# Joining the end of a mixture-of-experts layer with the node stage of a graph attention layer, on one core

## The chip, the cores and the metric

The kernel runs on 1 core of one Trainium2 chip. The metric is the device time of one execution in microseconds (us); lower is better. The kernel before took 6367.42 us, the median of three runs (6361.59, 6367.42 and 6380.49). The core has a matrix engine (TensorE, PE in the profile; PEld is its loading of weights), VectorE (DVE), ScalarE (ACT), GpSimd (POOL), a queue engine that mostly issues DMAs (SP), an on-chip memory of 128 partitions, and PSUM, eight banks into which TensorE writes.

## The reference, cut to what matters

The program is a graph network: a gated graph layer, a first feed-forward layer with 8 experts, a graph attention layer, and a second feed-forward layer. The change touches the end of the first feed-forward layer and the start of the attention layer, for N = 3125 nodes of 256 values each.

```
H = gelu(layernorm(x) @ W1 + b1)            # 3125 x 1024
probs = softmax(H @ Wg + bg); e = argmax(probs)
x = x + probs[e] * (H @ Wd[e] + bd[e])      # one expert of 8 for each node
# attention layer, start
y = layernorm(x)
h = einsum('ni,hio->nho', y, W)             # 8 heads of 32 values
# for each edge: lin = hs.a1 + hd.a2 + (hd-hs).a3 + |hd-hs|.a4 + (hs*hd).a5
```

The kernel needs for every node its row h and two groups of eight numbers, worked out from products of y with weights and from half of a5 * h * h. It keeps h also as the sum of three bf16 parts (high, mid, low), with which later matmuls pick rows of nodes.

## The kernel before, in words

The nodes lie in 25 blocks of 128 (the last has 53), one row of a block in each partition. All engines run one program in stages. Between stages stands a join: every engine waits for the last semaphores of the stage. Inside a stage each engine has a fixed order of instructions, written out by Python loops, and waits on counting semaphores.

Experts stage (3693 to 3908.6 us in the trace). A routing part sorts nodes by expert into 32 tiles of 128 slots. For each tile POOL gathers 128 rows of H from DRAM (L1654), PE transposes them (L1680), ACT and DVE each copy half to SBUF (L1712, L1737), PE multiplies them with the expert's weights (L1695), DVE copies the product from PSUM (L1744) and SP stores it to `expert_rows` (L1645). Then, block by block, PE turns the block's gates (L1700), ACT copies them (L1718), PE multiplies them with the 8 x 256 biases (L1704) and DVE adds the result to X (L1748). Beside that POOL gathers the block's rows back from `expert_rows` (L1664, four buffers) and DVE multiplies them with the probability and adds them to X (L1751). A join follows.

Nodes stage (3908.6 to 3997.3 us). SP first stores the list of edge slots (L1801), loads the layer's weights (L1802 to L1806), and then issues the 16 DMAs of L1809. Each copies one row of 6658 numbers of `edge_sources` into 8 partitions of the tile PEN, which is 128 x 6658 f32 in the end; nothing reads it before the next stage. Meanwhile DVE and ACT do the layer norm for all 25 blocks (L928, L931, L944, L933, L935, then L938 on DVE and L948 on ACT write Y). DVE works out coefficients from the weights (L1872 to L1893). Then a loop over blocks: PE transposes Y (L1822), ACT copies that (L1843), PE multiplies it with 272 columns of weights into one of two PSUM banks (L1831), ACT copies the row h to HB (L1847), POOL multiplies it with half of a5 (L1865) and with itself (L1867), DVE sums that by head (L1900) and finishes the sixteen numbers (L1903, L1904). SP stores the block's row to `gat_rows` (L1812). ACT writes the high part (L1851), DVE the rest (L1916), ACT the mid part (L1855), DVE the low part (L1909).

The next stage starts after a join on, among others, all 25 stores of rows, all 25 low parts and the 16 loads of PEN:

```
join([ns["stored"](16 * NB), ns["low"](NB), ns["pen"](256), ns["zero"](1), ns["weights"](1), ns["slots"](16)])
```

Its first instructions are ACT's DMAs of L2045 and POOL's gathers of L1978.

Of the kernel before, what the change touches and what calls it, by code (L numbers as in the profile page):

```python
# [8 lines left out]
ALU = mybir.AluOpType  # L9
# [5 lines left out]
NB = 25  # L15
# [1428 lines left out]
def hidden_memory(ar, panels):  # L1444

    m = Box()
    m.Y = ar.mk(NB, D)
    m.yT = [ar.mk(2, 512) for _ in range(2)]
    m.gt = ar.mk(NB, 8)
# [6 lines left out]
    m.gT = ar.mk(128)  # L1456
# [10 lines left out]
    m.bd = ar.mk(256)  # L1467
# [5 lines left out]
HIDDEN = {"w": 80, "wd": 128, "ln_step": NB + 1, "ln_var": NB, "ln_sd": 1, "ln_nb": 1, "y_v": 15, "y_a": 10,  # L1473
# [5 lines left out]
def hidden_weights(q, a, m, s):  # L1479
    q.dma_start(m.W1[:, :, :], a["W1"].rearrange("(k p) n -> p k n", p=128)).then_inc(s["w"].sem, 16)  # L1480
    q.dma_start(m.b1c, a["b1T"]).then_inc(s["w"].sem, 16)
    q.dma_start(m.Wg[:, :, :], a["Wg"].rearrange("(k p) n -> p k n", p=128)).then_inc(s["w"].sem, 16)
    q.dma_start(m.bg, spread(a["bg"])).then_inc(s["w"].sem, 16)
    q.dma_start(m.bd[0:8], a["bd"]).then_inc(s["w"].sem, 16)
# [12 lines left out]
def hidden_tensor(t, m, s, PS, ident):  # L1497
    for q in range(NG):
# [14 lines left out]
        t.wait_ge(*s["w"](80))  # L1513
# [54 lines left out]
def hidden_vector(v, m, cn, s, st, PS):  # L1568
    ln_vector(v, m.ln, s, m.Y, m.X)
    for q in range(NG):  # L1570
# [6 lines left out]
        v.wait_ge(*s["w"](80))  # L1577
# [30 lines left out]
    st.mark(v.tensor_tensor(m.gt, m.OH, over(m.pmx), ALU.mult))  # L1608
    v.wait_ge(st.sem, st.n)
# [6 lines left out]
NYG = 4  # L1616


def experts_memory(ar):
# [12 lines left out]
    m.yg = [ar.mk(256) for _ in range(NYG)]  # L1632
# [5 lines left out]
           "gt_ps": NB, "gt_sb": NB, "bd_ps": NB, "bd": NB, "yz": 1, "yg0": 112, "yg1": 96, "yg2": 96, "yg3": 96,  # L1638
           "x_new": NB}
# [8 lines left out]
def experts_gpsimd(g, m, cn, s, HR, YS0):  # L1648
    g.memset(m.yg[(NB - 1) % NYG], 0.0).then_inc(s["yz"].sem, 1)
# [6 lines left out]
    g.wait_ge(*s["pos"](1))  # L1656
    g.wait_ge(*s["yz"](1))
    for i in range(2):
        g.wait_ge(*s[f"st{i}"](256))
    for b in range(NB):  # L1660
        n = rows_of(b)
        if b >= NYG:
            g.wait_ge(*s["x_new"](b - NYG + 1))
        g.indirect_dma_start(m.yg[b % NYG][0:n], None, YS0[:, :],  # L1664
                             bass.IndirectOffsetOnAxis(ap=m.r.posi[0:n, b:b + 1], axis=0)).then_inc(s[f"yg{b % NYG}"].sem, 16)


def experts_tensor(t, m, h, cn, s, PS, eregs):
# [29 lines left out]
    t.wait_ge(*s["tok"](1))  # L1698
    for b in range(NB):
        t.transpose(PS[0:8, 6, 0:128], h.gt[:, b, :], cn.ident).then_inc(s["gt_ps"].sem, 1)  # L1700
        t.wait_ge(*s["gt_sb"](b + 1))
        if b:
            t.wait_ge(*s["bd"](b))
        t.matmul(PS[:, 7, 0:256], lhsT=h.gT[0:8], rhs=h.bd[0:8], start=True, stop=True).then_inc(s["bd_ps"].sem, 1)  # L1704


def experts_scalar(c, m, h, s, PS):
# [6 lines left out]
    for b in range(NB):  # L1714
        c.wait_ge(*s["gt_ps"](b + 1))
        if b:
            c.wait_ge(*s["bd_ps"](b))
        c.activation(h.gT[0:8], PS[0:8, 6, 0:128], ACT.Copy).then_inc(s["gt_sb"].sem, 1)  # L1718


def experts_vector(v, m, h, cn, s, st, PS):
# [10 lines left out]
    for i in range(NT0 + 1):  # L1732
# [6 lines left out]
        if i >= 1:  # L1739
# [4 lines left out]
            v.tensor_copy(m.og[j % 2], PS[:, 4 + j % 2, 0:256]).then_inc(s["og"].sem, 1)  # L1744
    for b in range(NB):
        n = rows_of(b)
        v.wait_ge(*s["bd_ps"](b + 1))
        v.tensor_tensor(h.X[:, b, :], h.X[:, b, :], PS[:, 7, 0:256], ALU.add).then_inc(s["bd"].sem, 1)  # L1748
        v.wait_ge(*s["bd"](b + 1))
        v.wait_ge(*s[f"yg{b % NYG}"](16 * (b // NYG + 1)))  # L1750
        v.scalar_tensor_tensor(h.X[0:n, b, :], m.yg[b % NYG][0:n], h.pmx[0:n, b:b + 1], h.X[0:n, b, :],  # L1751
                               ALU.mult, ALU.add).then_inc(s["x_new"].sem, 1)
# [19 lines left out]
def nodes_memory(ar):  # L1772
# [3 lines left out]
    m.A = ar.mk(248)  # L1776
    m.a45 = ar.mk(4)
# [4 lines left out]
    m.Y = ar.mk(NB, D)  # L1782
    m.Wa = ar.mk(2, 272)
    m.av5 = ar.mk(5, 256)
    m.msk = ar.mk(8)
    m.yT = [ar.mk(2, 128) for _ in range(2)]
    m.u1 = [ar.mk(256) for _ in range(2)]
    m.u2 = ar.mk(2, 256)
    m.hq = ar.mk(8)
    m.R = [ar.mk(NROW) for _ in range(2)]  # L1790
    m.ln = ln_memory(ar)
    return m


NODES = {"w": 80, "pen": 256, "ln_step": NB + 1, "ln_var": NB, "ln_sd": 1, "ln_nb": 1, "y_v": 15, "y_a": 10, "coef": 1,
         "zero": 1, "weights": 1, "slots": 16, "yt_ps": NB, "yt": NB, "rows_ps": NB, "rows": NB, "square": 2 * NB, "hq": NB, "logits": 2 * NB,
         "high": NB, "rest": NB, "mid": NB, "low": NB, "stored": 16 * NB}


def nodes_sync(q, a, m, L, s, HD, SEGD, SLD):  # L1800
    q.dma_start(SLD.rearrange("(r n) o -> r (n o)", r=104), L.slT[0:104]).then_inc(s["slots"].sem, 16)  # L1801
# [5 lines left out]
    for r in range(16):  # L1807
        row = SEGD[r * LROW:(r + 1) * LROW + 2, 0]
        q.dma_start(m.PEN[8 * r:8 * r + 8, :], row.unsqueeze(0).partition_broadcast(8)).then_inc(s["pen"].sem, 16)  # L1809
    for b in range(NB):  # L1810
        q.wait_ge(*s["logits"](2 * b + 2))
        q.dma_start(HD[b * 128:(b + 1) * 128, :], m.HB[:, b, 8:272]).then_inc(s["stored"].sem, 16)  # L1812


def nodes_tensor(t, m, s, PS, ident):
    for i in range(NB + 1):
        if i < NB:
            t.wait_ge(*ln_ready(s, i))
# [5 lines left out]
        if i >= 1:  # L1824
# [3 lines left out]
            if b >= 2:  # L1828
                t.wait_ge(*s["logits"](2 * b - 2))
            for k in range(2):  # L1830
                ins = t.matmul(PS[:, b % 2, 0:272], lhsT=m.yT[b % 2][:, k, :], rhs=m.Wa[:, k, :],  # L1831
# [4 lines left out]
def nodes_scalar(c, m, s, PS, epsc):  # L1836
    ln_scalar(c, m.ln, s, m.Y, m.X, epsc)
# [1299 lines left out]
```

## Time and profile before

| | |
|---|---|
| median of three runs | 6367.42 us (6361.59 to 6380.49) |
| the profiled execution | 6372.08 us, its span 6370.7 us |
| experts stage, tile loop | 3711 to 3858.8 us |
| experts stage, biases and gathers back | 3858.8 to 3908.6 us |
| nodes stage, layer norm and coefficients | 3908.6 to 3930 us |
| nodes stage, loop over blocks | 3930 to 3997.3 us |

Times inside the span are counted from its start. A row of the timeline tells the start, how long, the engine, the line of the kernel, the operation, what it writes and reads, how many were merged, and in brackets how long the engine had been idle and what released it. The granted clock (PEclk) is a share of TensorE's 2.4 GHz: 1.00 is 2.4 GHz and 0.50 is 1.2 GHz. "SPq" and "ACTq" are DMA issues; their time is the issue, not the transfer.

### The profile page before, as it was taken

The numbers are of one execution on the slowest core, as the hardware profiler recorded it, in microseconds if no ns is written. First come the engines' busy times: TensorE is split into PE (matmuls) and PEld (weight loads), VectorE is DVE, ScalarE is ACT, GpSimd is POOL, SyncE is SP. The second block draws the span as 40 slices with busy tenths as digits, with TensorE's granted clock in tenths as the row PEclk, the third lists the DMA queues.
The fourth block names the chain that finished last, engine by engine and source line by source line (L and its number), as shares of the span: only waits on it lengthen the run. The fifth ranks groups of instructions, "written<-read, shape, count | busy, mean of one in ns | idle before, by whom it ended". The sixth has DMA issues, their size and how long they took to land. (4 is left out here: it accounts for less than half of the span.)

```text
span 6370.7 us, 62334 instructions
## 1 busy us (share of the span) xinstructions
PE 4485.8 (70%) x17114; PEld 2672.2 (42%) x17114; DVE 2768.0 (43%) x6269; ACT 1760.5 (28%) x4039; POOL 2391.3 (38%) x2828
## 2 busy tenths in 40 slices
PE   1111314258999999999998986577777775997794
PEld 0010101024544544544444464455555554664462
DVE  7994000023263344353214035444444447777435
ACT  4331000000000000000001312345454455997121
POOL 3787777710000000000001013666666663886024
PEclk9999655579899999999999997688888887998697
DMA  8700122137432221322333133566666663776323
GB/s 356 286 1 25 58 75 75 58 125 260 137 110 92 89 96 71 111 83 74 109 111 105 66 125 90 174 201 199 196 197 202 196 195 99 241 242 215 116 63 107
DMA packets 381089, 865.14 MB, mean 136 GB/s; under 512 B 87347, under 2 KB 187733, under 8 KB 353370
## 3 DMA queue, kind: packets, MB, share of 16 engines
q1 hardware_dynamic: 250281, 686.15, 30.7%
q0 software_dynamic: 76816, 147.75, 9.0%
q10 hardware_dynamic: 53664, 27.26, 1.5%
q8 instruction: 159, 2.61, 0.2%
q14 instruction: 169, 1.38, 0.1%
HBM read 576.84 MB, written 284.11 MB: 135 GB/s over the span
## 5 line engine op out<-in xcount | busy, mean ns | idle before, releaser
L1110 PE MATMUL PS<-mem 128*128 128x512 f32 (+1 forms) x3500 | 1465.5, 575 | 392.4 <-issue 258.5
L1110 PEld LDWEIGHTS PS<-mem 128*128 128x128 f32 x3500 | 655.7, 201 | 1177.3 <-issue 1037.3
L1978 POOL DMA_INDIRECT mem<-gat_rows,mem x832 | 811.3, 975 | 479.9 <-issue 451.3
L1291 POOL TENSOR_TENSOR mem<-mem 128x256 f32<-128x256 f32 x25 | 19.9, 833 | 2140.5 <-DMA mem<-x 2140.5
L581 POOL DMA_INDIRECT adjacency_more<-mem x526 | 543.4, 1033 | 171.1 <-issue 171.1
L2086 DVE TENSOR_TENSOR mem<-mem,PS 128x512 f32<-128x512 f32 x416 | 285.7, 687 | 673.3 <-ACT mem L2059 516.2
L2021 PE MATMUL PS<-mem 128*128 128x256 bf16 x2496 | 437.1, 309 | 176.8 <-issue 163.3
L1176 ACT ACTIVATE mem<-PS 128x512 f32<-128x512 f32 (+1 forms) x35 | 19.0, 544 | 1918.0 <-PE PS L1110 1359.6
L2326 PE MATMUL PS<-mem 128*128 128x264 f32 x1660 | 461.6, 406 | 7.6 <-DVE mem L2283 3.1
L262 PE MATMUL PS<-mem 106*128 106x106 f32 (+4 forms) x446 | 102.0, 374 | 476.9 <-DVE mem L393 302.9
L1220 DVE COPY mem<-PS 128x512 f32<-128x512 f32 (+1 forms) x35 | 21.9, 625 | 954.0 <-PE PS L1110 651.3
L2059 ACT ACTIVATE mem<-PS,mem 128x256 f32<-128x256 f32 x832 | 424.1, 560 | 13.8
L2054 ACT ACTIVATE PS<-PS 128x512 f32<-128x512 f32 x416 | 245.2, 590 | 651.2 <-remote 507.8
L2021 PEld LDWEIGHTS PS<-mem 128*128 x2496 | 269.7, 109 | 276.7 <-issue 226.8
L581 POOL DMA_INDIRECT adjacency<-mem x256 | 347.3, 1357 | 95.4 <-issue 80.0
L2013 PE MATMUL PS<-mem 128*128 128x128 f32 x1664 | 311.0, 309 | 100.5 <-issue 77.8
L2326 PEld LDWEIGHTS PS<-mem 128*128 128x128 f32 x1660 | 283.3, 190 | 185.8 <-DVE mem L2283 92.8
L1993 PE MATMUL PS<-mem 128*128 128x256 f32 x832 | 330.7, 487 | 42.3 <-issue 34.9
L2283 POOL TENSOR_TENSOR mem<-mem 128x256 f32<-128x256 f32 x415 | 267.8, 645 | 166.6 <-ACT mem L2184 81.6
L2013 PEld LDWEIGHTS PS<-mem 128*128 128x128 f32 x1664 | 243.0, 162 | 168.0 <-issue 130.1
L1245 DVE TENSOR_TENSOR mem<-mem 128x2560 f32<-128x2560 f32 (+1 forms) x35 | 86.5, 2485 | 476.0 <-DMA mem<-adjacency_more 316.9
L2307 ACT ACTIVATE mem<-mem 128x128 f32<-128x128 f32 x830 | 287.9, 394 | 13.5
(398 smaller groups left out, 7033.3 us busy)
## 6 DMA issues: line engine op xcount, KB each, us to landing
mem<-adjacency SPq DMA_DIRECT2D x150, 1280.0 KB
gathered_rows<-mem SPq DMA_DIRECT2D x416, 264.0 KB
mem<-gathered_rows SPq DMA_DIRECT2D x208, 528.0 KB, 4.6
adjacency<-mem SPq DMA_DIRECT2D x56, 800.0 KB, 20.7
adjacency_more<-mem SPq DMA_DIRECT2D x56, 800.0 KB
mem<-adjacency_more SPq DMA_DIRECT2D x30, 1280.0 KB
adjacency<-mem SPq DMA_DIRECT2D x30, 1280.0 KB
mem<-edge_slots ACTq DMA_DIRECT2D x26, 1024.0 KB
```

The source lines that it names most:

```text
L581: g.indirect_dma_start(AD[:, :], bass.IndirectOffsetOnAxis(ap=aidx[:, k:k + 1], axis=0), SF[:, k:k + 1], None).then_inc(sc[f"{name}{n % 2} ...
L1110: ins = t.matmul(PS[:, f, 0:n], lhsT=h[:, b, f * 128:(f + 1) * 128], rhs=m.pan[i % NPAN][:, j, 0:n], start=(b == 0), stop=(b == NB - 1))
L1978: g.indirect_dma_start(m.Dg[i % RING][:, k, j, :], None, HD[:, :], bass.IndirectOffsetOnAxis(ap=L.idxD[:, c:c + 1], axis=0)).then_inc(s[f" ...
L1993: ins = t.matmul(PS[:, 7, 0:256], lhsT=nd.A[:, 120 - a:248 - a], rhs=m.x[p % NXD], start=(p % 16 == 0), stop=False)
L2013: t.matmul(PS[:, bank, f * 256 + e * 128:f * 256 + e * 128 + 128], lhsT=rows[:, e, f * 128:f * 128 + 128], rhs=cn.ident, is_transpose=True ...
L2021: t.matmul(PS[:, bank, f * 256:f * 256 + 256], lhsT=parts[:, bass.ds(at * 99 + (part * NROW + 8 + f * 128), 128)], rhs=slots, start=False, ...
L2054: c.activation(d, d, ACT.Abs).then_inc(s["ab"].sem, 1)
L2059: c.activation(m.by[n % 3][:, f * 256:f * 256 + 256], d[:, f * 256:f * 256 + 256], ACT.Identity, bias=nd.a45[:, f:f + 1], scale=nd.a45[:, ...
L2086: v.tensor_tensor(m.xx[n % 2], m.by[n % 3], PS[:, n % NDT, :], ALU.mult).then_inc(s["xx"].sem, 1)
L2283: return e.tensor_tensor(m.Wv[i % NOUT][:, j, 0:256].rearrange("p (f h d) -> p f h d", f=2, h=8), m.Dg[k % NDG][:, 2 * (i % 2) + j, 0:256] ...
L2307: c.activation(m.Ab[n % 2][:, j, :], cn.iota, ACT.Abs, bias=L.nsl[:, 2 * n + j:2 * n + j + 1]).then_inc(s["ab2"].sem, 1)
L2326: ins = t.matmul(PS[:, (6, 7, 0, 1)[i % NOUT], 0:264], lhsT=m.On[i % NOUT][:, j, :], rhs=m.Wv[i % NOUT][:, j, :], start=(j == 0), stop=(j ...
```

## The change

The two stages become one without a join between. The biases are no longer made by PE: a copy of all 8 x 256 biases is loaded into every partition before the tile loop, and DVE adds the right one while it evicts a tile's product; the tile's expert number is read into registers. In the new stage DVE adds a gathered block to X, works out its mean and variance at once, and the standard deviations are made for groups of five blocks. ACT alone writes Y. The squares of a row come from ACT, straight from PSUM, and POOL is left with one multiplication a block. There are six PSUM banks for products, four buffers for squares and rests, and 25 areas for gathered rows. These areas and the biases lie in tile AT, and some weights lie where PEN will be; so the 16 DMAs into PEN now stand behind the seventeenth store of rows and behind a wait for the last x_new. The coefficients are worked out in the tile loop, at its fifth step. The weights' loads stand ahead of the tile loop.

```
-            v.tensor_copy(m.og[j % 2], PS[:, 4 + j % 2, 0:256]).then_inc(s["og"].sem, 1)
+            if j % 8 == 0:
+                v.reg_load(regs, m.eo[0:1, j:j + 8])
+            e = v.snap(regs[j % 8], min_val=0, max_val=7 * 8)
+            v.tensor_tensor(m.og[j % 2], PS[:, 4 + j % 2, 0:256], nd.bd[:, bass.ds(e * 32, 256)],
+                            ALU.add).then_inc(s["og"].sem, 1)
+        if i == 4:
+            nodes_coefficients(v, nd, ns, st)
```

The loops for the biases on PE (L1700, L1704), ACT (L1718) and DVE (L1748) are removed, and in the hidden stage the load of the biases and one small multiplication on DVE (L1608).

```
+    m.yg = [m.AT[:, 256 * b:256 * b + 256] for b in range(NB)]
+    m.bd = m.AT[:, 0:2048]
+    m.av5 = m.PEN[:, 0:1280].rearrange("p (a b) -> p a b", a=5)
+NU = 4
+NBANK = 6
+ROWS_AT, REST_AT, LOW_AT = 9, 12, 15
+GATHERS_AHEAD = 10
...
+def nodes_sync(q, m, L, s, HD, SEGD, SLD):
     for b in range(NB):
         q.wait_ge(*s["logits"](2 * b + 2))
         q.dma_start(HD[b * 128:(b + 1) * 128, :], m.HB[:, b, 8:272]).then_inc(s["stored"].sem, 16)
+        if b == NB - ROWS_AT:
+            q.wait_ge(*s["x_new"](NB))
+            for r in range(16):
+                row = SEGD[r * LROW:(r + 1) * LROW + 2, 0]
+                q.dma_start(m.PEN[8 * r:8 * r + 8, :], row.unsqueeze(0).partition_broadcast(8)).then_inc(s["pen"].sem, 16)
...
 def nodes_tensor(t, m, s, PS, ident):
     for i in range(NB + 1):
         if i < NB:
-            t.wait_ge(*ln_ready(s, i))
+            t.wait_ge(*s["y"](i + 1))
             (transposes of block i; then, for i >= 1, the products of block i - 1)
...
 def nodes_scalar(c, m, s, PS, epsc):
+    deviations(0)
+    for i in range(NB + 8):
         if i < NB:
+            c.wait_ge(*s["nb"](i // 5 + 1))
+            c.activation(m.Y[:, i, :], m.X[:, i, :], ACT.Identity, bias=m.ln.nb[:, i:i + 1],
+                         scale=m.ln.sd[:, i:i + 1]).then_inc(s["y"].sem, 1)
             c.wait_ge(*s["yt_ps"](i + 1))
...
+            c.activation(m.HB[:, b, 8:264], PS[:, b % NBANK, 0:256], ACT.Copy).then_inc(s["rows"].sem, 1)
+            c.activation(m.u1[b % NU], PS[:, b % NBANK, 0:256], ACT.Square).then_inc(s["square"].sem, 1)
...
+        if i % 5 == 4 and i + 1 < NB:
+            deviations(i // 5 + 1)
...
+def nodes_gpsimd(g, x, m, s, es, YS0):
+    for b in range(NB + GATHERS_AHEAD):
+        if b < NB:
+            (gather block b, from b = 5 on after x_new of block b - 5)
+        if b >= GATHERS_AHEAD:
+            k = b - GATHERS_AHEAD
+            g.wait_ge(*s["square"](k + 1))
+            g.tensor_tensor(u, u, m.a5h, ALU.mult).then_inc(s["fifth"].sem, 1)
...
+def nodes_vector(v, h, m, s, es, PS):
+    for i in range(NB + LOW_AT):
+        (block i: x_new, bn_stats, bn_aggr; at i = 5, 10, ...: reciprocal and nb of a group)
+        (low part of block i - 15; sums and sixteen numbers of block i - 9; rest of block i - 12)
```

SP's order. Of the kernel before, from the last stores of the tile loop to the end of the nodes stage:

```order
L1645 DMA expert_rows<-mem 128x256 x32
L1801 DMA edge_slots<-mem 104x1024
L1802 DMA mem<-Wgat 128x2x256
L1803 DMA mem<-a 128x1280
L1804 DMA mem<-a4c 128x2
L1805 DMA mem<-a5c 128x2
L1806 DMA mem<-c_mask 128x8
L1809 DMA mem<-edge_sources 8x6658 x16
L1812 DMA gat_rows<-mem 128x264 x25
```

The same place of the changed kernel:

```order
L1785 DMA mem<-bd 128x2048
L1786 DMA mem<-Wgat 128x2x256
L1787 DMA mem<-a 128x1280
L1788 DMA mem<-a4c 128x2
L1789 DMA mem<-a5c 128x2
L1790 DMA mem<-c_mask 128x8
L1637 DMA expert_rows<-mem 128x256 x32
L1794 DMA edge_slots<-mem 104x1024
L1797 DMA gat_rows<-mem 128x264 x17
L1803 DMA mem<-edge_sources 8x6658 x16
L1797 DMA gat_rows<-mem 128x264 x8
```

The weights moved ahead of the stores of the tile loop, and the loads of `edge_sources` moved from ahead of all 25 stores of rows to behind the seventeenth.

ACT's order in the loop over blocks. Of the kernel before, a block's four instructions (turned Y, row, high part, mid part):

```order
L1843 ACTIVATE mem<-PS 128x256
L1847 ACTIVATE mem<-PS 128x256
L1851 ACTIVATE mem<-mem 128x264
L1855 ACTIVATE mem<-mem 128x264
L1843 ACTIVATE mem<-PS 128x256
```

Of the changed kernel, the deviations of a group (L1831) and one block (Y, turned Y, row, square, high part, mid part):

```order
L1831 ACTIVATE mem<-mem 128x5
L1837 ACTIVATE mem<-mem 128x256
L1842 ACTIVATE mem<-PS 128x256
L1846 ACTIVATE mem<-PS 128x256
L1849 ACTIVATE mem<-PS 128x256
L1854 ACTIVATE mem<-mem 128x264
L1858 ACTIVATE mem<-mem 128x264
```

Y of a block (L1837) and the square (L1849) moved into ACT's loop. PE's order in the loop is the same in both: two transposes of block i, then two products of block i - 1.

## Rows read from the trace of the kernel before

**Rows 1.** Windows: microseconds, busy of each engine (instructions), clock, DMA share, GB/s.

```profile
3858.80:3908.60 49.80, 36.48 (x74) 13.99 (x74) 22.62 (x51) 6.41 (x24) 24.46 (x25) 0.54 0.23 67
3925.70:3930.00 4.30, 0.00 (x1) 0.04 (x1) 4.09 (x12) 0.73 (x3) 0.00 (x0) 0.50 0.55 87
3955.00:3975.00 20.00, 14.02 (x51) 9.89 (x48) 12.76 (x40) 10.90 (x32) 12.56 (x16) 0.83 0.28 89
```

**Rows 2.** Timeline of the queue SP, 3680 to 4010 us.

```profile
3911.37 5.85 SPq L1809 DMA_DIRECT2D mem<-edge_sources  x16
```

**Rows 3.** Timeline, the last eviction, the first gathers, the end of the stage.

```profile
3858.40 0.42 DVE L1744 COPY mem<-PS 128x256 f32<-128x256 f32 x1 [3.04 <-PE PS L1695]
3861.29 0.95 POOL L1664 DMA_INDIRECT mem<-expert_rows,mem  x1 [21.68 <-DMA expert_rows<-mem]
3862.55 0.95 POOL L1664 DMA_INDIRECT mem<-expert_rows,mem  x1 [0.30 <-issue]
...
3864.12 0.49 DVE L1751 SCALAR_TENSOR_TENSOR mem<-mem 128x256 f32<-128x256 f32 x1 [4.14 <-DMA mem<-expert_rows,mem]
3864.53 0.42 DVE L1748 TENSOR_TENSOR mem<-mem,PS 128x256 f32<-128x256 f32 x1
...
3996.25 1.00 DVE L1909 TENSOR_TENSOR mem<-mem 128x264 bf16<-128x264 f32 x2
```

**Rows 4.** Timeline, the layer norm of the nodes stage.

```profile
3908.65 8.27 DVE L928 BATCH_NORM_STATS2 mem<-mem 128x6 f32<-128x256 f32 x25
...
3916.83 1.75 DVE L931 BATCH_NORM_AGGREGATE mem<-mem 128x2 f32<-128x6 f32 x25
...
3918.66 1.28 ACT L944 ACT_TABLE_LOAD   x1 [12.29 <-DVE mem L931]
...
3920.87 4.54 ACT L948 ACTIVATE mem<-mem 128x256 f32<-128x256 f32 x9 [0.60 <-DVE mem L935]
```

**Rows 5.** Source L948: instructions, ns minimum/median/maximum, first and last start.

```profile
L948 ACT ACTIVATE mem<-mem x40: 585/587/602, 556.5 to 5885.5; 128x256 f32<-128x256 f32 x40
```

**Rows 6.** Timeline of the loop over blocks, three places.

```profile
3931.94 0.63 PE L1822 MATMUL PS<-mem 128*128 128x128 f32 x2
...
3934.43 0.38 ACT L1847 ACTIVATE mem<-PS 128x256 f32<-128x256 f32 x1 [1.43 <-PE PS L1831]
...
3955.33 0.36 ACT L1843 ACTIVATE mem<-PS 128x256 f32<-128x256 f32 x1
...
3955.59 0.38 ACT L1847 ACTIVATE mem<-PS 128x256 f32<-128x256 f32 x1
...
3961.50 0.41 ACT L1855 ACTIVATE mem<-mem 128x264 bf16<-128x264 f32 x1
3961.82 0.37 ACT L1843 ACTIVATE mem<-PS 128x256 f32<-128x256 f32 x1
```

**Rows 7.** Windows, columns as in rows 1.

```profile
3866.00:3906.00 40.00, 32.52 (x65) 12.24 (x64) 19.28 (x43) 5.61 (x21) 20.67 (x21) 0.50 0.25 71
4009.00:4017.00 8.00, 4.40 (x23) 3.12 (x22) 7.36 (x5) 3.20 (x6) 7.70 (x2) 0.50 0.23 82
3930.00:3935.00 5.00, 4.82 (x12) 3.27 (x12) 0.65 (x3) 1.15 (x3) 1.57 (x3) 0.52 0.44 69
```

**Rows 8.** DMA issues, 3908 to 3998 us: KB each, median us to landing.

```profile
mem<-edge_sources SPq DMA_DIRECT2D x16, 208.1 KB
gat_rows<-mem SPq DMA_DIRECT2D x25, 132.0 KB, 1.8
```

**Rows 9.** Windows, columns as in rows 1.

```profile
3918.00:3919.00 1.00, 0.00 (x0) 0.00 (x0) 0.58 (x9) 0.34 (x1) 0.00 (x0) 0.50 0.53 80
3962.00:3963.00 1.00, 0.88 (x5) 0.51 (x3) 0.04 (x1) 0.49 (x2) 0.84 (x2) 0.97 0.08 23
```

**Rows 10.** Timeline of the tile loop.

```profile
3737.72 0.42 DVE L1744 COPY mem<-PS 128x256 f32<-128x256 f32 x1 [2.78 <-PE PS L1695]
...
3742.74 3.63 PE L1695 MATMUL PS<-mem 128*128 x16
```

More of the change, by code:

```diff
@@ L1637 @@
            "tr_ps": 2 * NT0, "cp_a": NT0, "cp_v": NT0, "mm": NT0, "og": NT0, "st0": 256, "st1": 256,
[L1638 to L1639 removed]
+           **{f"yg{i}": 16 * NB // NYG for i in range(NYG)}}
 def experts_sync(q, m, s, YS0):
@@ L1713, in experts_scalar, with experts_vector @@
                      ACT.Copy).then_inc(s["cp_a"].sem, 1)
[L1714 to L1721, printed above, removed]
+def experts_vector(v, m, h, nd, cn, s, ns, st, PS, regs):
     route_vector(v, m.r, cn, s, st, PS, h.OH)
@@ L1782, in nodes_memory, with nodes_weights @@
     m.Y = ar.mk(NB, D)
+    m.yT = [ar.mk(2, 128) for _ in range(2)]
+    m.u1 = [ar.mk(256) for _ in range(NU)]
+    m.hq = ar.mk(8)
+    m.R = [ar.mk(NROW) for _ in range(NU)]
+    m.ln = ln_memory(ar)
+    top, ar.top = ar.top, early
     m.Wa = ar.mk(2, 272)
-    m.av5 = ar.mk(5, 256)
+    m.a5h = ar.mk(256)
+    m.a45 = ar.mk(4)
     m.msk = ar.mk(8)
[L1786 to L1801, printed above, removed]
+    m.A = ar.mk(248)
+    early_end, ar.top = ar.top, top
+    return m, early_end
+NU = 4
+NBANK = 6
+ROWS_AT, REST_AT, LOW_AT = 9, 12, 15
+GATHERS_AHEAD = 10
+NODES = {"w": 80, "bias": 16, "pen": 256, "x_new": NB, "stats": NB, "mv": NB, "sd": 5, "rsd": 5, "nb": 5, "y": NB, "coef": 1, "half": 1,
+         "zero": 1, "weights": 1, "slots": 16, "yt_ps": NB, "yt": NB, "rows_ps": NB, "rows": NB, "square": NB, "fifth": NB,
+         "hq": NB, "logits": 2 * NB, "high": NB, "rest": NB, "mid": NB, "low": NB, "stored": 16 * NB}
+def nodes_weights(q, a, m, s):
+    q.dma_start(m.bd, spread(a["bd"].rearrange("e d -> (e d)"))).then_inc(s["bias"].sem, 16)
     q.dma_start(m.Wa[:, :, 0:256], a["Wgat"].rearrange("(k p) n -> p k n", p=128)).then_inc(s["w"].sem, 16)
@@ L1806, in nodes_sync @@
     q.dma_start(m.msk, a["c_mask"]).then_inc(s["w"].sem, 16)
-    for r in range(16):
-        row = SEGD[r * LROW:(r + 1) * LROW + 2, 0]
-        q.dma_start(m.PEN[8 * r:8 * r + 8, :], row.unsqueeze(0).partition_broadcast(8)).then_inc(s["pen"].sem, 16)
+def nodes_sync(q, m, L, s, HD, SEGD, SLD):
+    q.dma_start(SLD.rearrange("(r n) o -> r (n o)", r=104), L.slT[0:104]).then_inc(s["slots"].sem, 16)
     for b in range(NB):
@@ L1850, in nodes_scalar @@
             c.wait_ge(*s["logits"](2 * b + 2))
             c.activation(m.H3[:, b, 0:NROW], m.HB[:, b, 0:NROW], ACT.Copy, scale=-1.0).then_inc(s["high"].sem, 1)
[L1852 to L1853 removed]
+        if i >= 8:
+            b = i - 8
             c.wait_ge(*s["rest"](b + 1))
[L1855 to L1867 removed]
```

174 lines of the change are left out of this document (82 added, 92 removed).

## The prediction, made before the changed kernel ran

> **What bounds the kernel now.** I read the windows by stage first, then SP's timeline, the timeline at the borders of the stages, and last the DMA list. In the windows the reader is to see that from 3858.8 to 3908.6 us no engine is full: PE is busy 36.48 of 49.80 us and moves by turns with ACT and DVE, one block in some 1.9 us, and the granted clock is mostly the lower level [rows 1]. A whole stage of norm and coefficients with PE idle follows, then the loop over blocks [rows 1, 4]. The two stages run from the first gather back (3861.29) to the end of the last low part (3996.25 + 1.00 = 3997.25) [rows 3]: 136 us, of which the loop of biases is 47 and norm and coefficients are 21. These are what the change overlaps. SP's timeline has the second thing to see: the 16 loads of `edge_sources` are issued at 3911.37, ahead of all stores of rows [rows 2]. They are long. 16 times 208.1 KB [rows 8] is 3.41 MB, and with nothing else in flight the DMAs move 80 GB/s at a share of 0.53 [rows 9], that is 42.6 us. The share falls to 0.08 only at 3962 [rows 9], 50.6 us after the first issue, when the loads and the halves of stores that waited behind them are through. Now this is hidden: the compute ends 35 us later. The join waits for it, so what matters is when it starts.
>
> **Removed.** The bias work on PE, ACT and DVE and the join after it; DVE's adding moves into the eviction. The eviction stays a read of 256 columns of PSUM; a DVE addition with a PSUM operand of that shape (L1748) takes as long as the copy (L1744), 0.42 [rows 3], and DVE has idled 2.78 us before each eviction, waiting for PE [rows 10]. Eight registers read four times and one sum of registers a tile have no row here: below nothing they cannot go, and up to 2.7 us a tile they cost nothing. I take 0. If that cover were gone, each further us would be paid up to 32 times. The 4.09 us of coefficients [rows 1] move into the loop behind the eviction at 3737.72. They end at 3738.14 + 4.2 = 3742.3, DVE then still owes the next tile's copy, and PE wants it at 3742.74 [rows 10]: some 0.4 us late (an estimate), once. The small multiplication removed in the stage before (L1608) gives about that back. Together 0. The weights' loads lie beside the routing.
>
> **The new loop, by ACT.** DVE and POOL have less to do for a block than ACT, and ACT's order makes a circle with PE. PE's transposes of block i wait for Y of block i, which ACT now writes in the same turn; the products of block i - 1 are queued behind these transposes; and ACT's row copy of block i - 1 waits for these products. So a turn is: Y 0.59 [rows 5], a hand-over of 0.05 (an estimate), transposes and products at the lower clock from 3931.94 to 3934.43, 2.49 [rows 6], then row, square, high, mid, with starts 0.26 apart where PSUM is read and 0.32 where SBUF is [rows 6], together 1.16. That is 4.29 us a block, against some 2.4 in the loop before. Six banks don't help, as the wait isn't for a bank.
>
> When it starts: the first gather is issued at 3861.29, lands for DVE at 3864.12, and gathers are 1.26 apart [rows 3]; so the fifth is taken up at 3869.1, and with 0.49, 0.33 (8.27 over 25) and 0.07 and their waits the fifth variance is there at 3870.1. From the last variance to the first Y the norm took 3920.87 - 3918.58 = 2.29 us, a table load of 1.28 within [rows 4]. The first Y starts at 3872.4. At each later group ACT waits for DVE's part: 2.29 - 1.28, some 0.9 more. Block 1 starts at 3873.9; turns 1 to 4 are without high and mid (3.66), 5 to 7 without mid (3.97). That gives block 5 at 3889.4, block 8 at 3901.3, block 10 at 3910.8, block 15 at 3933.2, block 17 at 3941.7, block 24 at 3972.7. After block 24 the last row, square, POOL's product, sums, high, rest, mid and low take some 9 us more: compute ends at about 3981.4, 16 us earlier than now.
>
> **The load of PEN.** It stands behind the store of block 16. Its sixteen numbers need the square of turn 17: 3941.7 + 0.59 + 0.05 + 2.49 + 0.26 + 0.38 = 3945.5. POOL's multiplication takes 0.8 (12.56 over 16), DVE's three instructions 0.9 (0.32 each) [rows 1]. With the store's issue ahead, the first of the 16 DMAs goes at 3947.5, 36 us later than now [rows 2]. Then 1.8 us to the first landing (a store's median [rows 8]), 42.6 for the bytes, and the rest of the eight last stores, which stand behind in the same queue. Its lower bound is 47.5 us from issue to the end, its upper the 50.6 of now, in which small loads stood ahead. I take 48: the stage ends at 3995.5 where it ends now at 3997.25. The gain of 16 us is shut in behind the load.
>
> The sum: -1.8 us in the profiled execution of 6372.08 us, 6370.3. That execution lies 4.7 above the median; on the median of 6367.42 it is 6365.6.
>
> A rule speaks against this place of the load. The Trainium skill, "DMA: Bandwidth & Descriptors", section "Rules for kernel authors", says that an outermost dimension below 16 keeps a DMA on that many engines at most. The trace agrees: destinations of 8 partitions ran at a share of 0.53 [rows 9].
>
> **Rivals.** First, the faster clock. In the old loop PE had 2.4 GHz most of the time, 0.83 on average [rows 1]. If it had it here, transposes and products would shrink by up to half of 2.49, a turn to 3.1; over 17 turns that is 20 us, the load would be issued at 3927.5, and the stage would end at 3975.5: 6345.7. Against it stands what PE did at the lower clock. It is busy 2.5 of 4.29 us in a turn, 58%. It stayed at 0.50 through 40 us at 81% (products of 8 rows, though) and through 8 us at 55%, and rose after 4.82 of 5.00 us [rows 7]. The Trainium skill, "TensorE: Matmul & The Clock Gate", Part 1, has the clock fall only after an idle window; by that rule a loop without long gaps would keep the fast clock once it had it, and the time would be this rival's. The old loop's 0.83, with no long gap, is against that rule [rows 1].
>
> Second, the load is not the bound: it spreads over more DMA engines or is faster with fewer neighbours, and lands before 3981. It needs under 34 us where it took 42.6 at the least. Then the compute's end counts, 16 us earlier: 6351.5.
>
> Third, slower than before. If ACT does not overlap neighbours in this mix, row, square, high and mid cost their whole durations, 0.38, 0.38, 0.42 and 0.41, a turn takes 4.75, and block 17 starts 0.45 x 17 = 7.7 later; the load with it. The stage ends at 4003.2, 5.9 later than now: 6373.3. It decides from a turn of 4.4 us on, where the load's end passes 3997.3. Starts 0.26 and 0.32 apart in the trace speak against it [rows 6], DVE and POOL reaching for the same memory for it.
>
> **How the numbers follow.** Forecast 60%, faster clock 12%, load not the bound 8%, slower turn 15%; 5% for what I don't see, the tile loop above all. 0.3% is 19.1 us, about what a measurement of this kernel can tell from none. Faster by more: most of the faster clock and a little of the second, 10%. Slower by more: 4%, from the unseen. Within: 86%. The runs before spread over 19 us, so the median may be off by 5 either way. The range from 6349 to 6375 takes in the second and third rival and cuts off the first, with the rest of the tails. The likeliest case's own range, with the bounds 47.5 and 50.6 and a turn within 0.1, is 6360 to 6371.
>
> **What would show it.** Right: a granted clock near 0.50 from 3865 to the end of the stage; Y of neighbouring blocks 4.2 to 4.4 us apart and ACT idle before the turned Y and before the row, both for PE; the first load of `edge_sources` at 3947 to 3949; low parts done at 3980 to 3983 and then all engines idle for some 14 us until the first gather of the next stage near 3996. Wrong: the loads issued before 3935 or landed within 35 us, a clock above 0.7 in the loop, or a tile loop that ends later than 3859.

## The result and the profile after

Predicted was 6365.6 us, with a range of 6349 to 6375. The changed kernel took 6399.41 us (median of 20 runs, 6382.34 to 6411.21) where the kernel before, on the same chip, took 6381.51 (20 runs): a ratio of 1.0031, 95% interval 1.0024 to 1.0039. It is slower: the medians lie 17.9 us apart, the ratio makes it 19.8. The profiled execution took 6382.34 us, its span 6381.0.

Executions differ by up to 20 us in parts that the change doesn't touch, so I compare stretches, counted from the first gather back of POOL: 3861.29 in before [rows 3], 3869.21 here. First the queue SP and POOL's first gather of the next stage:

```profile
3886.72 78.49 SPq L1797 DMA_DIRECT2D gat_rows<-mem  x17
3965.26 5.40 SPq L1803 DMA_DIRECT2D mem<-edge_sources  x16
3970.70 31.60 SPq L1797 DMA_DIRECT2D gat_rows<-mem  x8
```
```profile
3869.21 0.95 POOL L1874 DMA_INDIRECT mem<-expert_rows,mem  x1 [21.88 <-DMA expert_rows<-mem]
...
4026.01 1.00 POOL L2013 DMA_INDIRECT mem<-gat_rows,mem  x1 [38.14 <-DMA gat_rows<-mem]
```

From the first gather back to the next stage's first gather are 4026.01 - 3869.21 = 156.8 us. In before it is

```profile
3998.03 1.01 POOL L1978 DMA_INDIRECT mem<-gat_rows,mem  x1 [5.06 <-DVE mem L1909]
```

3998.03 - 3861.29 = 136.7. The 20.1 us between them are the slowdown. The two profiled spans differ by only 10.3, since the first gather back came 7.9 later and the rest of the program, behind the stage, took 17.7 less than in the one trace of before (2355.0 against 2372.7; it is 2352 to 2361 in the eight other traces with spans near these).

The releaser changed too: in before DVE's last low part, now a DMA. The name in brackets is that of a store. By the packet records the last packet of the loads of `edge_sources` ends 152.6 us behind the first gather back, and the last packet of the stores that stand behind them in the queue 156.0. The windows (us, then busy of PE, PEld, DVE, ACT, POOL, then clock, DMA share, GB/s) show what these 38 us are:

```profile
3880.00:3986.00 106.00, 62.21 (x150) 37.52 (x150) 47.08 (x167) 49.99 (x139) 34.01 (x41) 0.50 0.25 58
3965.00:3995.00 30.00, 13.80 (x34) 8.42 (x32) 14.05 (x50) 15.53 (x44) 4.50 (x6) 0.56 0.58 84
3995.00:4012.00 17.00, 0.00 (x0) 0.00 (x0) 0.00 (x0) 0.00 (x0) 0.00 (x0) 0.50 0.52 67
```

The reader is to see three things: 106 us at a clock of 0.50; then, from 3995 on, no engine busy at all; and in that stretch a DMA share of 0.52, as in before with the loads alone (0.53), but 67 GB/s where it was 80 [rows 9]. Over all of the 3.41 MB it is 61 GB/s against 79: the loads take 55.7 us from their first packet's start to their last one's end, and 43.3 in before.

ScalarE's turns are the ones of the prediction. Its timeline:

```profile
3945.76 0.60 ACT L1837 ACTIVATE mem<-mem 128x256 f32<-128x256 f32 x1
3947.14 0.38 ACT L1842 ACTIVATE mem<-PS 128x256 f32<-128x256 f32 x1 [0.78 <-PE PS L1813]
3948.95 0.38 ACT L1846 ACTIVATE mem<-PS 128x256 f32<-128x256 f32 x1 [1.43 <-PE PS L1822]
3949.23 0.38 ACT L1849 ACTIVATE mem<-PS 128x256 f32<-128x256 f32 x1
3949.49 0.42 ACT L1854 ACTIVATE mem<-mem 128x264 bf16<-128x264 f32 x1
3949.81 0.42 ACT L1858 ACTIVATE mem<-mem 128x264 bf16<-128x264 f32 x1
3950.12 0.60 ACT L1837 ACTIVATE mem<-mem 128x256 f32<-128x256 f32 x1
```

From Y to Y 4.36 us, with two waits for PE in each, 0.78 and 1.43. Behind that comes DVE, in the iteration that makes the sixteen numbers of block 16:

```profile
3951.57 0.47 DVE L1915 SCALAR_TENSOR_TENSOR mem<-mem 53x256 f32<-53x256 f32 x1
...
3955.58 0.42 DVE L1951 SCALAR_TENSOR_TENSOR mem<-mem 128x264 f32<-128x264 f32 x1
3963.53 0.19 DVE L1924 RECIPROCAL mem<-mem 128x5 f32<-128x5 f32 x1 [7.52 <-ACT mem L1831]
...
3964.71 0.16 DVE L1944 SCALAR_TENSOR_TENSOR mem<-PS,mem 128x8 f32<-128x8 f32 x1
```
```profile
3963.20 0.30 ACT L1831 ACTIVATE mem<-mem 128x5 f32<-128x5 f32 x1
```

DVE idles 7.52 us for the standard deviations of the last group (L1831), which ACT writes at the end of turn 19. The sums of block 16 are queued behind that reciprocal (L1924).

### The profile page after: what moved, and what is told of

It is laid out like the page before. It is cut to its first block and busy times, and to the rows that moved or that the text cites. A ratio compares the mean times of both kernels' runs of the same rounds, so it can differ in the third digit from the quotient of the medians.

```text
span 6381.0 us, 62109 instructions
## 1 busy us (share of the span) xinstructions
PE 4445.4 (70%) x17039; PEld 2648.3 (42%) x17039; DVE 2750.3 (43%) x6236; ACT 1768.7 (28%) x4058; POOL 2374.8 (37%) x2802
## 5 line engine op out<-in xcount | busy, mean ns | idle before, releaser
L2056 PE MATMUL PS<-mem 128*128 128x256 bf16 x2496 | 423.6, 302 | 161.1 <-issue 142.2
```

Source lines behind the costliest of these rows:

```text
L2056: t.matmul(PS[:, bank, f * 256:f * 256 + 256], lhsT=parts[:, bass.ds(at * 99 + (part * NROW + 8 + f * 128), 128)], rhs=slots, start=False, ...
```

## The experiments

The table has one row for each profile. "Issue" is the first load of `edge_sources`, counted from the first gather back; "length" is from there to the next stage's first gather, where the loads and the stores behind them in the queue end last; "loads" is from the first packet's start of these loads to the last one's end; "stage" is from the first gather back to the next stage's first gather; "packet" is the median time of the 128 packets of 26,632 bytes of these loads, in the trace's packet records. The ratio is to the kernel before on the same chip, with its 95% interval.

```
kernel                                issue  length  loads  stage  packet  ratio
before                                 50.1  hidden   43.3  136.7   2.65   1
changed, first profile                 96.1   60.8    55.7  156.8   3.47   1.0031 (1.0024-1.0039)
changed, second profile                96.2   61.4    56.2  157.6   3.52   1.0050 (1.0030-1.0069)
loads behind block 14                  82.8   63.0    57.1  145.8   3.56   1.0012 (1.0003-1.0022)
loads at the tile loop's end           -0.8  hidden   61.6  164.7   3.22   1.0042 (1.0028-1.0055)
loads in 8 wide DMAs                   96.1  hidden   16.6  125.1   2.06   0.9983 (0.9970-0.9997)
ScalarE's Y first                      57.5   61.0    55.8  118.5   3.42   0.9968 (0.9956-0.9981)
before, loads late                    112.8   59.6    54.5  172.4   3.30   1.0065 (1.0039-1.0091)
before, biases at eviction             38.8  hidden   43.4  124.7   2.56   0.9982 (0.9962-1.0003)
Y first + wide                         57.4   22.4    16.6   79.8   2.06   0.9918 (0.9894-0.9942)
loads of 8 different rows              96.2   37.3    31.9  133.5   2.06   0.9994 (0.9980-1.0008)
a small load ahead of the loads        96.5   59.8    54.8  156.3   3.39   1.0036 (1.0019-1.0052)
Y first + wide + behind block 14       54.0   23.2    16.5   77.2   2.06   0.9900 (0.9878-0.9921)
Y first + wide + tile loop's end       -0.8  hidden   18.4   89.5   1.93   0.9913 (0.9894-0.9933)
```

**Loads behind block 14.**

```
-        if b == NB - ROWS_AT:
+        if b == NB - ROWS_AT - 2:
```

> Nothing is computed otherwise; SyncE issues the 16 loads of edge_sources behind the store of block 14 instead of block 16. Theory (the end is the issue of the loads plus their length): the last x_new is there in the changed kernel about 13 us before the loads are issued, so the issue moves from 3965 to about 3953, the stage ends some 12 us earlier, and the time is 10 to 13 us under the changed kernel, +6 to +10 us over the kernel before. Rival 1 (the circle of ScalarE and TensorE or the tile loop sets the end): no difference from the changed kernel, +18 to +20 us over the kernel before. Rival 2 (the loads are slow because stores and row work run beside them): issued earlier, more work lies beside them, they take over 65 us, and the gain is under 6 us.

The issue came 13.2 us earlier, the stage's end 11.0 (156.8 to 145.8). The theory holds: what is gained at the issue is gained at the end, less 2.2 us. The loads themselves took 1.4 of these longer (57.1 against 55.7), and the stores behind them the rest. Rival 2 is right in that and no more.

**Loads at the tile loop's end.** The two small tiles that shared PEN's place are kept elsewhere.

```
+    for i in range(2):
+        q.wait_ge(*es[f"st{i}"](256))
+    (the 16 loads)
     for b in range(NB):
```

> The loads of edge_sources are issued as soon as the tile loop's own stores are done (two small buffers that shared their place are moved), beside the gathers; nothing else is changed. Theory (the loads are all that keeps the stage's gain back): they end near 3935, hidden, the compute's end at about 3993.5 in the changed kernel's time counts and the stage ends some 30 us earlier: 28 to 32 us under the changed kernel, 9 to 13 us under the kernel before. Rival 1 (the loads do not bind): as the changed kernel, +18 to +20 us. Rival 2 (the loads beside the gathers hold these up, since both use the 16 DMA engines): the gathers come more than 1.3 us apart, the first Y is later than 9.4 us behind the first gather by several us, and the time is between +0 and -8 us.

Rival 2 held, and far beyond what I gave it. DVE's additions of gathered blocks and, below them, POOL's gathers:

```profile
3908.79 0.49 DVE L1914 SCALAR_TENSOR_TENSOR mem<-mem 128x256 f32<-128x256 f32 x1 [22.18 <-DMA mem<-expert_rows,mem]
...
3913.28 0.49 DVE L1914 SCALAR_TENSOR_TENSOR mem<-mem 128x256 f32<-128x256 f32 x1 [3.32 <-DMA mem<-expert_rows,mem]
...
3920.51 0.49 DVE L1914 SCALAR_TENSOR_TENSOR mem<-mem 128x256 f32<-128x256 f32 x1 [6.06 <-DMA mem<-expert_rows,mem]
```
```profile
3889.15 0.95 POOL L1873 DMA_INDIRECT mem<-expert_rows,mem  x1 [21.88 <-DMA expert_rows<-mem]
...
3909.55 0.95 POOL L1873 DMA_INDIRECT mem<-expert_rows,mem  x1 [14.43 <-DVE mem L1914]
```

The first gathered block reaches DVE 19.6 us after its gather's issue (2.8 in before [rows 3]), the next ones 4.5 and 7.2 us later each; and the first Y, 10.5 us behind the first gather in the changed kernel, comes after 49.9:

```profile
3939.06 0.60 ACT L1836 ACTIVATE mem<-mem 128x256 f32<-128x256 f32 x1 [4.75 <-DVE mem L1926]
```

The 32 us of waiting at the end are gone, and 39.5 came in ahead: 164.7 against 156.8. So the gathers' short packets wait while the long ones are under way.

**Loads in 8 wide DMAs.** The same rows, by destination partitions r x 8 + e: one DMA for each e, with 16 partitions and 16 rows, instead of one for each row r.

```
+            for e in range(8):
+                src = bass.AP(SEGD.tensor, SEGD.offset, [[LROW, 16], [1, LROW + 2]])
+                q.dma_start(m.PEN[e:128:8, :], src).then_inc(s["pen"].sem, 16)
```

> The same 3.41 MB at the same place, but in 8 DMAs with 16 destination partitions each instead of 16 with 8. Theory (a destination of 8 partitions keeps a DMA on 8 of the 16 DMA engines, and the engines' rate on these long packets is the limit): the load takes 25 to 35 us instead of 60, the stage ends 25 to 32 us earlier or at the compute's end: 22 to 32 us under the changed kernel, -4 to -13 us against the kernel before. Rival (the source in memory, or the loading of one address over and over, is the limit): the length stays within 50 to 60 us, and the time is within 5 us of the changed kernel, +14 to +20.

```profile
3960.00:3976.00 16.00, 9.07 (x23) 5.82 (x24) 5.39 (x20) 8.14 (x23) 2.90 (x4) 0.50 0.97 206
```
```profile
3986.64 1.00 POOL L2013 DMA_INDIRECT mem<-gat_rows,mem  x1 [6.37 <-DVE mem L1932]
```

206 GB/s at a share of 0.97, and DVE's low part is the releaser again, as in before. The stage is 125.1 us, 31.7 less. That is the compute's own length, since the loads are hidden: their last packet ends 114.0 us behind the first gather back.

**ScalarE's Y first.**

```
     deviations(0)
+    normed(0)
     for i in range(NB + 8):
         if i < NB:
-            (Y of block i)
             (turned Y of block i)
+        if i + 1 < NB:
+            normed(i + 1)
...
-        if i % 5 == 4 and i + 1 < NB:
+        if i % 5 == 3 and i + 2 < NB:
```

> Only the order on ScalarE is changed: it writes Y of block i + 1 right behind the turned Y of block i, before the row of block i - 1, so that TensorE has its next transposes' input while ScalarE copies and squares rows. Theory (a turn of 4.36 us is the circle Y, transposes, turned Y and products): a turn falls to about 2.7 to 3.2 us, TensorE's busy share rises, the 16 loads of edge_sources are issued some 20 to 28 us earlier, and the time is 20 to 28 us under the changed kernel, 0 to -10 us against the kernel before. Rival (ScalarE is bound by its own instructions, as overlap among them is poor in this mix): a turn stays over 4 us and the time as in the changed kernel, +15 to +20. Of the clock: if it rises over 0.5 in the loop, the turn shrinks under 2.7.

```profile
3890.49 0.61 ACT L1835 ACTIVATE mem<-mem 128x256 f32<-128x256 f32 x1
3890.98 0.39 ACT L1851 ACTIVATE mem<-PS 128x256 f32<-128x256 f32 x1
3891.25 0.40 ACT L1854 ACTIVATE mem<-PS 128x256 f32<-128x256 f32 x1
3891.51 0.45 ACT L1859 ACTIVATE mem<-mem 128x264 bf16<-128x264 f32 x1
3891.82 0.44 ACT L1863 ACTIVATE mem<-mem 128x264 bf16<-128x264 f32 x1
3892.14 0.40 ACT L1845 ACTIVATE mem<-PS 128x256 f32<-128x256 f32 x1
3892.40 0.63 ACT L1835 ACTIVATE mem<-mem 128x256 f32<-128x256 f32 x1
```
```profile
3865.00:3912.00 47.00, 31.51 (x118) 20.68 (x119) 41.75 (x144) 35.90 (x108) 31.88 (x35) 0.85 0.32 96
3940.00:3973.00 33.00, 0.00 (x0) 0.00 (x0) 0.00 (x0) 0.00 (x0) 0.00 (x0) 0.50 0.49 70
```

The last line of the edit makes a group's deviations one turn sooner, as Y is written one turn sooner. The turn shown is 1.91 us without any wait, the plain sum of ACT's six starts. Others wait for PE or, at a new group, for DVE: the mean from block 5 to block 24 is 2.30 us, against 4.43 in the changed kernel. The granted clock is 0.85 on average where it had been 0.50, so the order and the clock both have a share in this; the shown turn is shorter than the 2.49 us that PE's part of a turn takes at the lower clock [rows 6]. Together they cost about half of each turn, more than I expected. The loads went 38.5 us earlier. They still took 61.0, and the engines stood idle for them from before 3940 to 3973.

**Before, loads late.** The kernel before, with the 16 loads moved behind `if b == 16:` in the loop of stores and nothing else.

> The kernel before, with one thing alone: the 16 loads of edge_sources are issued behind the store of block 16 instead of ahead of all stores. Theory (the place of the loads costs by itself): they are issued near 3974, and the stage ends 50 to 60 us later, at 4024 to 4034, where it ended at 3997: +27 to +37 us over the kernel before. It tells also what lengthens the packets of 26,632 bytes: if they take 2.4 to 2.8 us as in the kernel before, +27, it is something of the changed kernel's program; if 3.4 to 3.6 as in the changed one, +35, it is the place behind the stores (when and behind what the queue starts them). Rival (a late load is hidden by something else): within 5 us of the kernel before.

```profile
3751.03 5.43 SPq L1813 DMA_DIRECT2D mem<-edge_sources  x16
```
```profile
3810.67 1.01 POOL L1979 DMA_INDIRECT mem<-gat_rows,mem  x1 [40.74 <-DMA gat_rows<-mem]
```

The stage is 35.7 us longer. The loads take 54.5 us where they took 43.3, with this one edit, on a program that is otherwise that of before (and 43.4 in the kernel before with the biases at eviction, on the same chip): the lengthening belongs to the loads' place, not to the new stage's program.

**The changed kernel again, and a small load ahead.** The second of these puts one 4 KB load of the mask right ahead of the 16 loads.

> The changed kernel itself, on the chip of this group and with a second profile. Theory: the loads of edge_sources take 58 to 62 us from first issue to the next stage's first gather again (60.8 in the first profile, 50.6 in the kernel before), so the length belongs to the kernel; the time is +18 to +22 us over the kernel before. Rival (it was that execution's disturbance): the length is near 50 us in this profile, and the time +8 to +12.

> The changed kernel with one more load of 4 KB (the mask, once more) right ahead of the 16 loads of edge_sources, as they have one ahead of them in the kernel before, where their packets of 26,632 bytes took 2.65 us against 3.5 in the changed kernel. Theory C (what stands right ahead in the queue sets which engines they get or how the packets lie to one another): length 50 us, 8 to 10 us under the changed kernel. Theory D (the stores further ahead set it, or the ones behind): length 58 to 62 us, no difference.

The length belongs to the kernel (61.4 us). Theory D holds: a small load right ahead changes next to nothing (59.8 us, 3.39 a packet).

**Loads of 8 different rows.** Still 16 DMAs of 8 partitions.

```
+            for h in range(2):
+                for e in range(8):
+                    rows = bass.AP(SEGD.tensor, SEGD.offset + 8 * h * LROW, [[LROW, 8], [1, LROW + 2]])
+                    q.dma_start(m.PEN[64 * h + e:64 * h + 64:8, :], rows).then_inc(s["pen"].sem, 16)
```

> The changed kernel, with the loads of edge_sources still 16 DMAs of 8 destination partitions, but each DMA takes 8 different rows of the source, where now its 8 partitions all take the same row. Bytes, place, count and number of partitions are as they were. Theory A (8 partitions keep a DMA on 8 engines, and each engine has its own limit): length 58 to 62 us as now, time as the changed kernel. Theory B (8 engines that read the same row at the same moment hold each other up): packets fall from 3.5 us to about 2.1, as in the run with 16 partitions of 16 different rows, the length to 34 to 38, and the time to 20 to 26 us under the changed kernel.

```profile
3951.45 9.46 SPq L1804 DMA_DIRECT2D mem<-edge_sources  x16
```
```profile
3988.77 1.00 POOL L2014 DMA_INDIRECT mem<-gat_rows,mem  x1 [14.70 <-DMA gat_rows<-mem]
```
```profile
3961.00:3984.00 23.00, 7.67 (x19) 4.60 (x17) 9.92 (x34) 10.85 (x31) 3.09 (x4) 0.57 0.56 130
```

Theory B has the numbers right: packets of 2.06 us instead of 3.4 to 3.6, 37.3 us instead of 60.8, at a share of 0.56 and 130 GB/s in a window in which the last stores run too. Its mechanism isn't shown by them, since the edit changes two things. Each DMA reads eight rows instead of one, and its eight partitions lie 8 apart instead of side by side; no run has one without the other. Two other loads in the trace of the changed kernel speak against the reading. First `bd` (L1785), which gives all 128 partitions the same 8192 bytes, then `x_kept` near the end of the program, 128 partitions of 25,600 different bytes, some gathers beside it:

```profile
3701.00:3704.00 3.00, 0.61 (x2) 0.08 (x1) 2.04 (x9) 0.00 (x0) 0.00 (x0) 0.50 0.89 325
6290.00:6299.00 9.00, 0.00 (x0) 0.00 (x0) 0.00 (x0) 0.00 (x0) 6.68 (x7) 0.50 0.97 378
```

By the packet records their median packets take 0.309 and 0.954 us, which is 26.5 and 26.8 GB/s for one DMA engine. Reading one row for all partitions, then, goes as fast as reading different rows, and the 2.06 us of these loads (12.9 GB/s) are half that rate even with different rows. That leaves the place of the destination partitions as a rival that no run has tested: all 128 in one DMA, 8 apart, side by side is the order of the three speeds.

So two things made the loads long: one row into eight neighbouring partitions, against eight rows into partitions 8 apart, a factor of about 1.7 in a packet; and half the engines with 8 partitions, a factor of two in the whole (31.9 us here, 16.6 with 16 partitions, at the same 2.06 a packet).

**Before, biases at eviction.** The first part of the change alone: the addition with a register address at the eviction, as in the changed kernel; no bias work on PE, ACT and DVE beside the gathers; the rest is the kernel before.

> The kernel before with the first part of the change alone: expert biases added at eviction in the tile loop, and no transposes, products, copies and additions for them beside the gathers; norm, coefficients and the loop over blocks stay stages of their own. Theory: the stretch from the first gather to the last x_new, 47 us, falls to 25 gathers 1.25 apart, 31.3, and 3.3 behind the last, about 34.5: 12 to 14 us under the kernel before, less 0.6 us for the tile loop's later start. Rival 1 (the 32 evictions with register addresses hold up the tile loop): each tile over 4.34 us apart, 0 us or a loss. Rival 2 (without the products between them the norm starts on a colder clock or the gathers are slower in a row): a gain under 8 us.

```profile
3637.84 0.95 POOL L1663 DMA_INDIRECT mem<-expert_rows,mem  x1 [21.82 <-DMA expert_rows<-mem]
...
3667.84 1.57 POOL L1663 DMA_INDIRECT mem<-expert_rows,mem  x1 [0.30 <-issue]
```
```profile
3669.34 0.48 DVE L1742 SCALAR_TENSOR_TENSOR mem<-mem 128x256 f32<-128x256 f32 x1 [0.76 <-DMA mem<-expert_rows,mem]
```

The stretch to the last x_new is 32.0 us, the stage 12.0 shorter, as the theory has it. The time's interval reaches from -0.4% to nothing, so by the time alone this stays unclear.

**Combinations.** They use the edits shown above.

> The changed kernel with both edits that helped alone: ScalarE writes Y of block i + 1 right behind the turned Y of block i, and the loads of edge_sources go in 8 DMAs of 16 partitions. Theory (stage end = the later of the compute's end and issue + length of the loads): loads issued 28.8 us behind the first gather's 30 (as in the run with the order alone, 57.5 us behind the first gather), 27 to 29 us long, end 85 to 87 us behind the first gather where it was 118.5 with the order alone and 157 in the changed kernel: 31 to 34 us under the run with the order alone, 45 to 55 us under the kernel before. Rival (the loads were slow because they ran alone, and beside the faster loop and its stores they slow these down or are slowed): length over 40 us, gain over the kernel before under 42 us.

> ScalarE's new order, the loads of edge_sources in 8 DMAs of 16 partitions, and these issued behind the store of block 14 instead of 16. Theory (the end of the stage is still issue + length, 10.4 us after the compute's end in the run with the first two): a block takes some 2 us in that loop, so the loads go 4 us earlier, and the time is 3 to 5 us under the run with the first two, -53 us against the kernel before. Rival (the loads now get among the stores and the last gathers and hold up the loop): no difference or a loss.

> ScalarE's new order, the 8 wide loads, and these issued at the tile loop's end beside the gathers. Theory (long packets in the DMA engines hold up the gathers' short ones: with the narrow loads 5 gathers' transfers took 20 us and more each instead of 3): the wide loads last 17 to 25 us, the first x_new waits for most of that, and the stage ends some 17 to 22 us after what its compute alone would need (some 69 us behind the first gather with the fast loop), 86 to 92 us behind the first gather: 2 to 12 us slower than the wide loads behind block 16. Rival (with wide loads the gathers pass between them): first Y within 5 us of its time without loads, and the stage 75 us, 5 to 8 us faster than the run with the first two.

The first gave 79.8 us for the stage, 5 us under what I worked out. I had taken 27 to 29 us for the length from the run with wide loads alone, where the compute ended last; it was 22.4, of which the loads themselves are 16.6 in both. The second gave 77.2, 2.6 less; it has the best ratio, 0.9900 (0.9878 to 0.9921): 6290.46 us against 6353.20. That is faster than both kernels. The intervals of the first two overlap, so that the second beats the first is told by the stage alone. The third, with the wide loads beside the gathers, is 12.3 us longer in the stage than the second and 9.6 in the medians: even 18.4 us of long packets are better put where no gather waits. What ends the second now:

```profile
3905.99 4.99 SPq L1803 DMA_DIRECT2D mem<-edge_sources  x8
3911.02 13.35 SPq L1797 DMA_DIRECT2D gat_rows<-mem  x10
```
```profile
3920.78 0.73 POOL L1885 TENSOR_TENSOR mem<-mem 128x256 f32<-128x256 f32 x1 [0.28 <-ACT mem L1854]
3929.18 1.00 POOL L2018 DMA_INDIRECT mem<-gat_rows,mem  x1 [7.68 <-DMA gat_rows<-mem]
```

The loads' last packet ends 71.8 us behind the first gather back. The ten stores behind them move their packets only from 71.0 on and end at 76.2, and DVE's last low part ends at 75.4 (3926.35 + 1.11 - 3852.02). Compute and queue are nearly level, and moving the loads further has little left to gain.

## Why the prediction was wrong, step by step

- **What bounds the stage: right.** "The gain of 16 us is shut in behind the load." The loads and the stores behind them ended last, and the compute had been done for 32 us.
- **Tile loop at nothing: nearly.** From PE's first product of the routing to the first gather back it took 3869.21 - 3699.91 = 169.3 us, in before 3861.29 - 3693.47 = 167.8: 1.5 more.

```profile
3699.91 1.03 PE L1319 MATMUL PS<-mem 128*128 128x200 f32 x2 [5.13 <-DVE mem L1604]
```
```profile
3693.47 1.03 PE L1319 MATMUL PS<-mem 128*128 128x200 f32 x2 [5.54 <-DVE mem L1610]
```
```profile
3733.98 0.43 DVE L1719 TENSOR_TENSOR mem<-PS,mem 128x256 f32<-128x256 f32 x1 [6.37 <-issue]
```

  The first eviction with its registers waited 6.37 us on "issue"; later ones keep the 4.34 of before.
- **Turn, clock and start: right.** First Y 11.1 us behind the first gather predicted, 10.5 measured; a turn 4.29, measured 4.36; Y of block 17 at 80.4, measured 80.9; the clock 0.50 from before the first Y to 3986. ScalarE's two waits in a turn are those named.
- **When the loads are issued: the step that failed first.** "Its sixteen numbers need the square of turn 17", so 3947.5, which is 86.2 us behind the first gather. It was 96.05, 9.8 late. Block 16's square was there, but DVE works in program order: block 16's sums stand in iteration 25, behind the reciprocal of the last group, and that waits for ACT's deviations, written at the end of turn 19. I had counted DVE's three instructions and not what is queued ahead of them. With the loads behind block 14, whose sums stand ahead of that reciprocal, they went at 82.8, right behind the last x_new (3951.57 + 0.47 - 3869.21 = 82.8 in the changed kernel).
- **How long they take: the step that failed worst.** I took 48 us, with bounds of 47.5 and 50.6 "of now". It was 60.8. Counted to the next stage's first gather, which is 0.8 behind the end of the stage in before, my 48 are 48.8; the excess is 60.8 - 48.8 = 12.0 us, and with the 9.8 above this is all of the 21.8 us between 135.0 predicted and 156.8 measured for the stage. The term that was mis-sized is "42.6 for the bytes": the loads take 43.3 us in before, but 55.7 here. The rest of the 48 was about right: 0.9 to the first packet where I took 1.8, and 3.4 for the stores behind where 3.6 were left. The bytes, the partitions and the share of 0.53 were the same; a packet took 3.47 us instead of 2.65. The bound from both sides was none: it was one measurement in one place of the queue, and the kernel before with only the loads moved has 59.6. Why a packet takes longer in that place stays open.
- **The rival of the slower turn** came out on the right side by the wrong mechanism: ScalarE's turn is 4.36, under the 4.4 from which it decides, and row, square, high and mid start 0.26 to 0.32 apart as in before [rows 6].
- **The compute's end:** predicted 120.1 us behind the first gather, measured 3992.37 + 1.11 - 3869.21 = 124.3. It decided nothing.
- **The rival of the faster clock: right to give it little.** In the circle PE was busy 62.21 of 106 us and stayed at 0.50. With the circle broken it was busy 31.51 of 47 and had 0.85. But the loop didn't have the fast clock when it began. The tile loop ends at 1.00, and the clock fell while PE stood idle for the first gathered blocks:

```profile
3869.00:3872.00 3.00, 0.00 (x0) 0.00 (x0) 0.00 (x0) 0.00 (x0) 2.18 (x3) 0.65 0.17 46
3872.00:3880.00 8.00, 0.00 (x0) 0.00 (x0) 7.19 (x21) 0.64 (x2) 6.17 (x7) 0.50 0.37 109
```

  The Trainium skill, "TensorE: Matmul & The Clock Gate", Part 1, has the clock fall only after an idle window; the trace agrees in this place. Whether a loop would keep the fast clock "once it had it", as the prediction draws from that rule, this run doesn't test. The run with ScalarE's Y first does in part: the clock stood at 1.00 for 10 to 14 us at a time, with gaps on PE of up to 1.3 us, and was back at 0.50 each time behind PE's longer wait at a new group of five, 2.2 to 3.2 us. The first of these waits in the shown loop:

```profile
3886.52 0.69 PE L1813 MATMUL PS<-mem 128*128 128x128 f32 x2 [2.16 <-ACT mem L1835]
```

- **The rival that the load isn't the bound** had the right lever (DMAs over more engines), which this kernel doesn't pull. The rule that I weighed, the Trainium skill's "DMA: Bandwidth & Descriptors", "Rules for kernel authors", agrees with the runs: 8 destination partitions gave a share of 0.52, 16 gave 0.97.

What the idea itself was worth can now be told. With the loads hidden the changed program's stage is 125.1 us against 136.7, of which the biases alone bring 12.0. So merging norm and loop brought next to nothing by itself, as the circle's 4.36 us a block took back what it saved; with the circle broken as well, the stage is 77.2.

## What to carry to other kernels

A transfer that was hidden becomes the bound as soon as it is moved behind the work it used to hide behind: follow its issue through the program order of every engine ahead of it, and take its length in its old place as one measurement, not as a range. When an engine writes the input of another one's next step and reads its last result in one turn, write the input first. For rows that go to several partitions, let each DMA reach at least 16 partitions that lie apart: here 16 partitions 8 apart took 16.6 us where 8 side by side took 55.7.

## What the runs showed of the hardware that I had not expected

- Eight neighbouring partitions loaded from the same 26.6 KB row took 2.56 to 3.56 us a packet (medians), eight that lie 8 apart, from different rows, 2.06, with the same share of the DMA engines (0.52 and 0.56). With 16 partitions 8 apart it was 2.06 too, 206 GB/s. All of these are slow beside the 0.954 us of a 25,600-byte packet of `x_kept` in the same program. That one row is read by many isn't enough for it: `bd`, one row into 128 partitions, ran at full rate.
- The same loads of equal rows had packets of 2.56 to 2.65 us in the two kernels where small loads stand ahead and stores behind, and 3.2 to 3.6 in all others: behind stores of rows, or at the tile loop's end beside the gathers. A small load right ahead didn't bring the shorter time back. What it is about the place is open. From the second round on, eight packets start spread over 2.3 to 2.5 us in before; in the changed kernel they start within 0.5 us in the second to fifth round and within 1.1 to 1.4 later. That would fit engines that hold each other up in lockstep; it is argued, not shown.
- Long packets beside gathers delayed the first gathered block from 2.8 to 19.6 us, and to 8.1 with the wide loads (18.4 us of them).
- Four of the runs (the changed kernel's second profile, before with the loads late, before with the biases at eviction, and Y first + wide) fell on a chip where the kernel before took 5895.81 us, against 6353 to 6382 elsewhere, at a mean granted clock of 0.889 to 0.897 in the profiled executions against 0.855 to 0.871. The stage here, most of it bound by DMA and hand-overs, took the same there (157.6 against 156.8). The ratios in the table are each within one chip.
